# A different issue order for the value matmuls of an attention kernel, and own tables of order for its first and last image

## The reference

```python
wp = normalize_weight(w_proj)[:, :, 0, 0] / fan_in        # 1536 x 512
wo = normalize_weight(w_out)[:, :, 0, 0] / fan_in         # 512 x 512
xf = x.reshape(B, C, N)                                   # 16 x 512 x 1024
h = jnp.einsum('oc,bcn->bno', wp, xf)
qkv = h.reshape(B, N, n_heads, 3 * d_k)                   # 8 heads of 64
q, k, v = jnp.split(qkv, 3, axis=-1)
q = pixnorm(q) * scale; k = pixnorm(k) * scale; v = pixnorm(v)
attn = jnp.einsum('bihd,bjhd->bijh', q, k)
attn = jax.nn.softmax(attn, axis=2)
res = jnp.einsum('bijh,bjhd->bihd', attn, v).reshape(B, N, C)
res = jnp.einsum('oc,bnc->bon', wo, res).reshape(B, C, H, W)
return (a_c * x + b_c * res) / div
```

## Time and profile before

| | |
|---|---|
| median of three runs | 2993.76 us |
| the profiled execution | 2993.77 us, its span 2992.0 us |
| granted TensorE clock | 1.000 on the mean |
| TensorE matmuls busy | 2934.9 us, 98% |
| TensorE weight loads busy | 2014.0 us, 67% |
| VectorE busy | 2582.7 us, 86% |
| ScalarE busy | 2381.6 us, 80% |
| GpSimd busy | 456.2 us, 15% |

### The profile page before, as it was taken

One profiled execution on the slowest core, in us unless ns is written; L12 is line 12 of the kernel. 1 busy time (PEld: TensorE's weight loads), 2 busy tenths in 40 slices (PEclk: granted clock), 3 DMA queues, 4 the chain that ended last, 5 costly groups with the idle time before them and its releaser, 6 DMA issues.

```text
span 2992.0 us, 85444 instructions
## 1 busy us (share of the span) xinstructions
PE 2934.9 (98%) x36928; PEld 2014.0 (67%) x36928; DVE 2582.7 (86%) x3197; ACT 2381.6 (80%) x2993; POOL 456.2 (15%) x678
## 2 busy tenths in 40 slices
PE   7999999999999999999999999999999999999997
PEld 5676666766667667676666766666666666766664
DVE  6998888988889888898888988888898888988896
ACT  6887778878778778787787878788787778878785
POOL 0210121101211111112111211012110121101210
PEclk9999999999999999999999999999999999999999
DMA  3233414233242332333323333332422424233234
GB/s 99 49 55 67 90 32 109 49 82 76 44 96 52 78 79 50 87 62 79 69 58 78 62 80 67 68 72 58 97 56 63 91 39 107 51 70 88 35 77 100
DMA packets 459531, 211.04 MB, mean 71 GB/s; under 512 B 407954, under 2 KB 407954, under 8 KB 459154
## 3 DMA queue, kind: packets, MB, share of 16 engines
q1 hardware_dynamic: 459152, 205.58, 32.3%
HBM read 71.30 MB, written 33.55 MB: 35 GB/s over the span
## 4 chain that ended last, share of the span: by engine, by line
PE 78%; DVE 8%; POOL 5%; ACT 4%; issue 3%; DMA 3%; SPq 0%; ACTq 0%; DVEq 0%; POOLq 0%
PE ps_pv L930 20%; PE ps_score L909 18%; PE ps_dense L887 11%; PE ps_dense L889 10%; PE ps_dense L891 10%; DVE probs L722 4%; PE ps_dense L946 3%; PE ps_dense L948 2%; PE ps_dense L947 2%; DMA x_raw<-in_x 2%; POOL rs_t L369 1%; POOL rs_t L367 1%; POOL rs_t L371 1%; ACT e_tile L528 1%; ACT probs L535 1%
## 5 line engine op out<-in xcount | busy, mean ns | idle before, releaser
L722 DVE TENSOR_TENSOR probs<-e_tile,probs 128x1024 f16<-128x1024 f32 x1024 | 1241.3, 1229 | 71.0 <-ACT probs L535 64.8
L528 ACT ACTIVATE e_tile<-ps_score,shift 128x1024 f32<-128x1024 f32 x1024 | 1106.0, 1117 | 234.4 <-PE ps_score L909 135.2
L930 PEld LDWEIGHTS ps_pv<-v_pair,probs 128*128 128x128 f16 x24576 | 772.0, 98 | 187.4 <-issue 108.6
L930 PE MATMUL ps_pv<-v_pair,probs 128*128 128x65 f16 (+1 forms) x24576 | 821.5, 193 | 7.2 <-DVE probs L722 5.6
L909 PE MATMUL ps_score<-qkT 64*128 64x512 f16 x6144 | 753.9, 378 | 4.0 <-ACT e_tile L528 3.7
L887 PE MATMUL ps_dense<-wpT_hi,x_hi 128*128 128x512 f32 x1536 | 621.1, 404 | 1.8 <-DVE wpT_lo L793 1.5
L889 PE MATMUL ps_dense<-wpT_lo,x_hi 128*128 128x512 f32 x1536 | 600.0, 391 | 0.0
L891 PE MATMUL ps_dense<-wpT_hi,x_lo 128*128 128x512 f32 x1536 | 599.2, 390 | 0.0
L535 ACT ACTIVATE probs<-e_tile 128x1024 f16<-128x1024 f32 x512 | 542.6, 1060 | 21.4 <-PE ps_pv L930 2.1
L909 PEld LDWEIGHTS ps_score<-qkT 64*128 64x128 f16 x6144 | 257.0, 94 | 363.3 <-issue 90.7
L713 DVE CAST probs<-e_tile 128x1024 f16<-128x1024 f32 x512 | 359.4, 702 | 68.3 <-PE ps_pv L930 65.7
(11 more groups left out here) (50 smaller groups left out, 1737.0 us busy)
## 6 DMA issues: line engine op xcount, KB each, us to landing
x_raw<-in_x SPq DMA_DIRECT2D x128, 256.0 KB, 3.3
x_res<-in_x SPq DMA_DIRECT2D x128, 256.0 KB, 3.9
out<-x_res SPq DMA_DIRECT2D x128, 256.0 KB, 2.5
arena<-in_w_proj SPq DMA_DIRECT2D x24, 128.0 KB, 2.9
qkT<-arena SPq DMA_TRANSPOSE x128, 4.7
resT<-res_split SPq DMA_TRANSPOSE x128, 3.6
arena<-in_w_out SPq DMA_DIRECT2D x1, 1024.0 KB, 5.7
```

The lines of the kernel that those rows point to most:

```text
L528: act.activation(e_tile[:, t % E_BUFS, :, :], ps_score[:, t % 2, :, :], ACT.Exp, bias=shift[:, 0:1], scale=1.0 / (QK_UP * QK_UP)).then_inc ...
L722: dve.tensor_tensor(probs_of(b, t, 1), e_tile[:, t % E_BUFS, :, :], probs_of(b, t, 0), ALU.subtract).then_inc(probs_low, 1)
L930: mm = pe.matmul(ps_pv[:, h, o:o + n], probs_of(b, t, part)[:, h, queries], v[:, cols], start=(j == 0 and it == 0 and part == 0 and cols.s ...
```

## The change

Two things. In attend the loop over the three products now stands outside the loop over the four query tiles: the same 24 matmuls of a slot with the same operands, in another order. And the tables of order are three dictionaries, FIRST for image 0, LAST for image 15 and STEADY for the rest. An image is 64 x 1024 ticks long now, and STEADY holds the old entries times 16, apart from the two bank tables, in which 0 and 1 have changed places. FIRST and LAST hold the same names with other numbers, FIRST also those for the weights. timeline collects all ticks of all images, sorts them by absolute tick and then by image, and issues their tasks. bank_free is replaced by take_bank, which remembers the last user of each bank.

```diff
-TICKS = 64
+TICKS = 1024
-SCORE_AT = (-37, 197, 291, 387, 882, 921, 935, 1255, 1422, 1602, 1717, 1824, 1887, 2052, 2198, 2243, 2271,
...
+STEADY = {
+    "SCORE_AT": (-592, 3152, 4656, 6192, 14112, 14736, 14960, 20080, 22752, 25632, 27472, 29184, 30192, 32832,
...
+LAST = {
+    "SCORE_AT": (-616, 32, 3925, 9176, 14160, 14704, 14912, 18840, 23178, 25536, 28224, 30162, 30966, 31770,
...
+        def tables(b):
+
+            return FIRST if b == 0 else LAST if b == B - 1 else STEADY
+
+        def timeline(task, names):
+
+
+            plans = [{name: at(tables(b).get(table, ())) for name, table in names.items()} for b in range(B)]
+            moments = {(SLOTS * TICKS * b + tick, b, tick) for b in range(B) for found in plans[b].values()
+                       for tick in found}
+            for _, b, tick in sorted(moments):
+                task(b, tick, plans[b])
...
-            def bank_free(b, s, bank):
...
+            bank_left = {}
+
+            def take_bank(bank, emptied, count):
+
+                if bank in bank_left:
+                    pe.wait_ge(*bank_left[bank])
+                bank_left[bank] = (emptied, count)
...
-                        for it in range(4):
-                            queries = slice(it * P, (it + 1) * P)
-                            o = it * SUMS
-                            for part, cols in ((0, slice(0, SUMS)), (0, slice(LOW, LOW + D)), (1, slice(0, SUMS))):
-                                n = cols.stop - cols.start
+                        for part, cols in ((0, slice(0, SUMS)), (0, slice(LOW, LOW + D)), (1, slice(0, SUMS))):
+                            n = cols.stop - cols.start
+                            for it in range(4):
+                                queries = slice(it * P, (it + 1) * P)
+                                o = it * SUMS
                                 mm = pe.matmul(ps_pv[:, h, o:o + n], probs_of(b, t, part)[:, h, queries], v[:, cols],
```

More of the change, by code:

```diff
@@ L384, in task @@
                     norms(b, g)
-            timeline(pool, task, steady, opening)
+            timeline(task, names)
         @block.sync
@@ L483, in square @@
                 after(act, reduced, 24 * b + n - 1)
[L484 removed]
+                act.activation(squares[:, n % 2, :], ps_dense[:, tables(b)["PROJ_BANK"][n], :], ACT.Square).then_inc(squared, 1)
             def copy_proj(b, n):
@@ L620, in task @@
                     high_x(b, piece)
-            timeline(act, task, steady, opening)
+            timeline(task, names)
         @block.vector
@@ L828, in task @@
-            def task(b, s, when):
-                if when is opening:
-                    for c in when["w_norm"].get(s, ()):
-                        norm_weights(c)
-                    for m in when["w_scale"].get(s, ()):
-                        scale_weights(m)
-                    for m in when["w_low"].get(s, ()):
-                        low_weights(m)
+            names = dict(take="TAKE_AT",
+                         low_res="LOW_RES_AT",
+                         add="ADD_OUT_AT",
+                         reduce="REDUCE_AT",
+                         seed="SEED_AT",
+                         scale="SCALE_AT",
+                         low_v="LOW_V_AT",
+                         low_qk="LOW_QK_AT",
+                         low_x="LOW_X_AT",
+                         cast="HIGH_P_AT",
+                         low_p="LOW_P_AT",
+                         w_norm="W_NORM_AT",
+                         w_scale="W_SCALE_AT",
+                         w_low="W_LOW_AT")
@@ L836, in task @@
+            def task(b, s, when):
+                for c in when["w_norm"].get(s, ()):
+                    norm_weights(c)
+                for m in when["w_scale"].get(s, ()):
+                    scale_weights(m)
+                for m in when["w_low"].get(s, ()):
+                    low_weights(m)
                 for u in when["take"].get(s, ()):
@@ L858, in task @@
                     split_probs_low(b, t)
-            timeline(dve, task, steady, opening)
+            timeline(task, names)
         @block.tensor
         def _(pe):
-            def bank_free(b, s, bank):
-                users = [(tick, proj_copied, 24, n + 1) for n, tick in enumerate(PROJ_AT) if PROJ_BANK[n] == bank]
-                users += [(tick, out_added, 8, k + 1) for k, tick in enumerate(OUT_AT) if OUT_BANK[k] == bank]
-                past = [(tick + SLOTS * TICKS * e, copied, per, count, e) for tick, copied, per, count in users
-                        for e in range(-2, 3) if tick + SLOTS * TICKS * e < s
-                        and not (isinstance(b, int) and not 0 <= b + e < B)]
-                if past:
-                    tick, copied, per, count, e = max(past, key=lambda u: u[0])
-                    pe.wait_ge(copied, per * (b + e) + count)
+            bank_left = {}
[3 more added lines that the diff above has]
+                bank_left[bank] = (emptied, count)
             def project(b, n):
@@ L882, in project @@
                     pe.wait_ge(w_low, GROUP_UNITS * (g + 1))
-                bank = PROJ_BANK[n]
-                bank_free(b, PROJ_AT[n], bank)
+                bank = tables(b)["PROJ_BANK"][n]
+                take_bank(bank, proj_copied, 24 * b + n + 1)
                 pix, cols = slice(nt * P, (nt + 1) * P), slice(g * GROUP_O, (g + 1) * GROUP_O)
@@ L940, in project_out @@
                     pe.wait_ge(res_turned[half], 16 * 4 * (b + 1))
-                bank = OUT_BANK[k]
-                bank_free(b, OUT_AT[k], bank)
+                bank = tables(b)["OUT_BANK"][k]
+                take_bank(bank, out_added, 8 * b + k + 1)
                 rows = slice(k % CT * P, (k % CT + 1) * P)
```

345 lines of the change are left out of this document (166 added, 179 removed), and 45 rows, old and new, of tables (EXP_AT, FIRST, HIGH_P_AT, LAST).

## The result

| | before | changed |
|---|---|---|
| median of the runs, us | 2994.11 (12 runs, 2990.79 to 2995.84) | 2987.86 (12 runs, 2986.32 to 2988.75) |
| ratio, 95% interval | | 0.9979, 0.9972 to 0.9986 |
| profiled span, us | 2992.0 | 2987.0 |

The change gains 6 us (4 to 8 by the interval) where 32 were forecast. That is what rival R1 gave (2988.8).

What follows compares the result with a forecast made beforehand. TensorE was taken to bound the kernel from image to image. From the 2992.0 us span, 27 (matmul order), 2 (head) and 3 (tail) came off, giving 2960; with 1.8 us outside the span 2961.8, predicted as 2962, range 2953 to 2991.

Steps and rivals of the forecast that it cites:

- R1: Rival: new matmul order worth nothing, 30.2 ns belongs to load and matmul pair; only tables count, 2988.8 us; chance 0.28.
- part 1: Reordered value matmuls in attend: no neighbours adding onto the same columns; 29 us, 27 us left after deductions.
- the term of 29 us: Value matmuls: 24,576 steps falling from 30.2 to 29.0 ns once the stalls vanish.
- the middle bound: Value matmuls at columns plus 2.5 ns, as 512-column output matmuls show: 29.4 ns a step, gain 19 us.
- R2: Rival: value matmul step falls only to columns plus 2.5 ns; 2971.8 us; chance 0.12.
- Head: First image's new table: -2 us, bounds 4 gained and 3 lost; transposes at about 15 us, first projection near 21.
- From 100 to 160 us: First image, where first scores meet projections: TensorE idle 2.5 of 60 us, new order to take 1.5 us of it.
- Tail: Last image's new table, alternating scores and value blocks plus a rearranged end: -3 us.
- The stretch ahead: Last image before its very end: work moved ahead of 2880 us helps VectorE; -1 us, bounds -6 and +3.
- The end: First output projection ahead of the last two value blocks; chain of stores and loads ends 1.6 to 2 us earlier.
- R4: Rival: slower by tables, first output projection waits for the seventh unit's transpose; 2998 to 3002 us; chance 0.04.
- Tables together: New tables for first and last image, head -2 and tail -3: -5 us.

Runs made afterwards that it cites:

- e13: Kernel before with 48 columns instead of 65 and 64 in the value matmuls of seven of eight key blocks (output wrong): 2958.1 us, one run.
- e1: Kernel before with only the new loop order in attend: 2994.79 us, ratio 0.9999 to before.
- e3: Changed kernel with the old loop order, the new table for the first image and the common one for the last: 2996.35 us, ratio 0.9999 to before.
- e2: Changed kernel with the old loop order put back, so both new tables alone: 2989.00 us, ratio 0.9978 to before.
- e4: Changed kernel with the old loop order and old head order, so the last image's new table alone: 2988.70 us, ratio 0.9978 to before.
- e9: e4 with the end of the last image's order put back (five table numbers): 2990.79 us, ratio 0.9989 to before.
- e10: Kernel before with only the end of the last image's order changed: 2992.13 us, ratio 0.9991 to before.
- e8: Kernel before with value weight loads of 64 columns instead of 128 in seven of eight key blocks (output wrong): 3066.3 us, one run.

## Why the forecast was right or wrong

**What bounds the kernel.** Right on the bound, TensorE by 182.4 of 184 us. Wrong, as it seems, on pricing the steps at full value because "the 22 us by which VectorE is under TensorE in each image cover the rest": e13 got 2.6 of 6.7 us, 3.3 at most without the lower clock. At 2.6 of 6.7 us, 1.17 ns less in 1,536 steps, 1.8 us per image, would have been 0.7 us, some 11 us in all. This is an estimate from one run with a saving nearly four times as large; a smaller one may come back more fully, which no run tested. So part 1 probably had two faults, and the second may have cost up to half of the 27 us even if the first had not been made.

**Part 1, the step that failed.** It is the term of 29 us, and the sentence under it: "I take that as the cause: writing again what was just written costs, the cost gathers for some matmuls and is paid in one stall." The term measured nothing (e1, 0.9999; the period 183.97 us instead of 183.85, where about 182 was forecast). The rows were right (plain steps of 29 ns, stalls of 7, none ahead of a first product); what they meant was not. The stalls fell on fixed places of a regular pattern, and their place within three products was read as their reason. With the order turned they fell on first products too, and with all tiles on the same columns nothing became dearer. The price of the pair is its columns and about 3 ns, whatever its neighbours write. The 2.5 ns of the earlier trace rows, which I had as the middle bound, was the better sign: nearly the same addition on matmuls of 512 columns, where no stall can be blamed. Held against 30.2 it left 0.8 ns, which didn't come either (R2), and what I had against R1, that no stall comes ahead of a first product, was one pattern counted 4,248 times and not so many proofs. Its own counter-argument, that blocks with different patterns have the same mean, was in the text and was right. (One count was off without weight: from 2900 to 2962 us stand 812 value matmuls; about 1,008 is the number of all matmuls there, which makes 0.2 us.)

**Head.** Forecast -2, measured 0 (e3), with an interval that still holds -2. First transposes 17.04 instead of 15 (16.1 in e2 and e3), first projection 23.22, outside "20 to 22". What was missed is the table load of 1.28 us, which needs a place of its own when the first activation of an engine changes. The splits of x were named with 0.69 us each but counted as made good by the earlier transposes; their copies, which now stand ahead of the last weight copy on ScalarE, were not named. From 100 to 160 us, where 1.5 us were to come, TensorE is idle for 2.2 of 60 us instead of 2.5.

**Tail.** Forecast -3, measured -6.6 (e4), each term in the right place and too small. The stretch ahead, forecast -1 with bounds of -6 and +3, is the one mis-sized most: -3.1 us in e9's trace, -3.8 by the medians. That only work moved ahead of 2880 us can help was right, and more was moved than the term held. The end, forecast -1.6 to -2, gave -2.4 us by e10's medians and -3.2 in its trace. Its 2.6 us of projection stand in the traces; the 0.7 of delay can't be told from none there. The 0.9 to 1.1 us by which the chain of stores and loads itself got shorter were not in the sum. "Over 1 us" for the last transpose was low (2.1 us relative to the last value matmul, 3.7 absolute), and its reason was half of the truth: in the kernel before, the low half on VectorE stood behind the second addition and came last. It changed nothing in the time, since the transpose isn't on the chain that ends last. In the changed kernel it even stands ready from 2963.2 us and waits on SyncE, behind two stores and a load, until 2965.64. R4 didn't come: the first output projection met no wait for its transpose; the only one for resT is 1.12 us at 2969.67.

**The numbers.** Tables together: forecast -5, measured -6. That these two are so near is in part luck: the head gave nothing where -2 was forecast, and the tail gave twice its term. All of the miss, 26 of 32 us, is part 1. R1, to which I gave 0.28, is what happened.

## What to carry to other kernels

Here a regular stall in a stream of equal instructions told where a deficit was paid, not who caused it. Compare the mean step with that of other widths before pricing a cause, and ask whether the width alone gives it. A step saved on the bounding engine is worth its full price only where the engines that feed it could already run faster in the same places; idle time summed over a period doesn't show that. At the end of a kernel follow the chain that ends last and take out of it what can run sooner: here a few moved tasks, above all one output projection put ahead of the last two value blocks, gave 2 to 4 us, about as much as the new order of a whole image. And hold one profile against several of the same order before reading a microsecond in its head.

## What was not expected of the hardware

- A pair of a 128-column fp16 load and a matmul took 25.2 ns at 32 and at 48 columns alike, while the records show each load as 96 ns: by these two numbers some four loads overlap.
- A load of half the columns was slower: 111.5 ns in the records against 97.7, step 31.6 against 30.2 ns (e8).
- In the head the projections' matmuls of 512 columns start 427 ns apart, 1.2 GHz, before they start 227 apart, though the granted clock of those slices reads 1.00 in all of them. In the kernel before nine did so (to 25.0 us), in the changed one thirteen (to 28.9), after 2.17 us of idle behind the transposes instead of 1.50. That idle time doesn't set the number: e3, with the same 2.17, has six, and e1, with 1.50, seven. Four more at 0.2 us are 0.8 us of the changed head in this profile. Rows of the changed kernel at either level:

```profile
24.21 0.63 PE L934 MATMUL ps_dense<-wpT_hi,x_lo 128*128 128x512 f32 x1
24.64 0.63 PE L930 MATMUL ps_dense<-wpT_hi,x_hi 128*128 128x512 f32 x1
...
29.54 0.40 PE L930 MATMUL ps_dense<-wpT_hi,x_hi 128*128 128x512 f32 x1
29.77 0.39 PE L932 MATMUL ps_dense<-wpT_lo,x_hi 128*128 128x512 f32 x1
```
